# Corner weights in PSUM, all squares on the scalar engine, the offset chain spread over tiles, and a looped gather program that copies its indices per tile

## What is computed

```python
x = x + _L0_conv_ref(_gn(x), W, b)                    # attention over all pixels: relu(f'f)^2, values normalised
x = x + _L1_conv_ref(_gn(x), offset_w, offset_b, dcn_w)   # modulated deformable convolution, 9 taps
x = x + _L2_conv_ref(_gn(x), ...)                     # diagonal LSTM in both directions
x = x + _L3_conv_ref(_gn(x), ...)                     # adaptive deformable convolution, 9 taps
```

## Time and profile before

| | before |
|---|---|
| runs, us | 14,493.77, 14,497.03, 14,500.39 (median 14,497.03) |
| profiled execution, us | 14,491.91; span of the trace 14,489.8 |
| PE busy | 8644.1 us, 60% |
| POOL busy | 8632.6 us, 60% |
| DVE busy | 6885.5 us, 48% |
| ACT busy | 4883.7 us, 34% |

### The profile page before, as it was taken

One profiled execution on the slowest core, in us unless ns is written; L12 is line 12 of the kernel. 1 busy time (PEld: TensorE's weight loads), 2 busy tenths in 40 slices (PEclk: granted clock), 3 DMA queues, 4 the chain that ended last, 5 costly groups with the idle time before them and its releaser, 6 DMA issues. The chain is left out here.

```text
span 14489.8 us, 110898 instructions
## 1 busy us (share of the span) xinstructions
PE 8644.1 (60%) x26294; PEld 3625.3 (25%) x26294; DVE 6885.5 (48%) x8889; ACT 4883.7 (34%) x7671; POOL 8632.6 (60%) x7465
## 2 busy tenths in 40 slices
PE   7888887878788787852188888233332323333322
PEld 2333333323233333321044444111111111111111
DVE  3444545454544545444344444444454454444444
ACT  4444443434344444431178888111111111111100
POOL 0176775757576675767500000477777777777777
PEclk9899898989899898975599999555555555555555
DMA  0122222222222222227522222634343443433332
GB/s 7 37 84 78 87 82 82 82 81 82 81 82 81 83 84 80 85 84 175 139 56 56 58 56 56 127 98 115 97 114 101 114 114 99 115 98 98 97 94 88
DMA packets 1168915, 1277.68 MB, mean 88 GB/s; under 512 B 795967, under 2 KB 924415, under 8 KB 1164671
## 3 DMA queue, kind: packets, MB, share of 16 engines
q0 software_dynamic: 338688, 925.30, 21.6%
q1 hardware_dynamic: 815710, 347.84, 10.5%
q10 hardware_dynamic: 14368, 3.21, 0.1%
HBM read 1080.00 MB, written 195.82 MB: 88 GB/s over the span
## 5 line engine op out<-in xcount | busy, mean ns | idle before, releaser
L423 POOL DMA_INDIRECT b_gathered<-table,b_iu x3528 | 4451.0, 1262 | 1323.9 <-issue 988.5
L423 POOL DMA_INDIRECT d_gathered<-table,d_iu x3528 | 4114.3, 1166 | 1279.1 <-issue 1049.6
L518 PE MATMUL PS<-b_key 128*128 (+1 forms) x5600 | 2557.9, 583 | 18.2 <-ACT b_weights L694 7.3
L543 PE MATMUL PS<-ident,d_sample 128*128 128x128 f32 (+1 forms) x1960 | 504.2, 421 | 3229.5 <-DVE d_sample L893 2996.5
L694 ACT ACTIVATE b_weights<-PS 128x896 f32<-128x896 f32 (+1 forms) x1400 | 1281.8, 916 | 2296.3 <-PE PS L518 1886.3
L531 PE MATMUL PS<-b_weights,b_values 128*64 128x448 f32 (+1 forms) x5600 | 1466.7, 591 | 619.0 <-DVE b_weights L873 585.0
L881 DVE TENSOR_TENSOR d_gathered<-d_gathered,d_w 128x2304 f32<-128x2304 f32 x392 | 1002.6, 2558 | 1494.8 <-DMA d_gathered<-table,d_iu 1451.8
L881 DVE TENSOR_TENSOR b_gathered<-b_gathered,b_w 128x2304 f32<-128x2304 f32 x392 | 1002.2, 2557 | 1395.2 <-DMA b_gathered<-table,b_iu 1391.5
L704 ACT ACTIVATE d_sampleT<-PS 128x512 f32<-128x512 f32 x392 | 233.2, 595 | 3346.0 <-PE PS L543 2676.3
L518 PEld LDWEIGHTS PS<-b_key 128*128 128x128 f32 (+1 forms) x5600 | 994.5, 197 | 1330.5 <-issue 1325.1
L873 DVE TENSOR_TENSOR b_weights<-b_weights 128x896 f32<-128x896 f32 x672 | 731.2, 1088 | 1185.2 <-ACT b_weights L694 943.3
(11 more groups left out here) (224 smaller groups left out, 9533.6 us busy)
## 6 DMA issues: line engine op xcount, KB each, us to landing
b_gathered<-table,b_iu POOLq DMA_INDIRECT x3528
d_gathered<-table,d_iu POOLq DMA_INDIRECT x3528
l_x_and_h<-xs SPq DMA_DIRECT2D x224, 224.0 KB, 3.6
hs<-l_hT SPq DMA_DIRECT2D x224, 224.0 KB, 2.4
d_h<-hs SPq DMA_DIRECT2D x32, 1554.0 KB
table<-b_table_rows SPq DMA_DIRECT2D x208, 128.0 KB, 1.9
table<-d_table_rows SPq DMA_DIRECT2D x208, 128.0 KB
xs<-b_key SPq DMA_DIRECT2D x14, 1568.0 KB
```

Source lines behind the costliest of these rows:

```text
L423: pool.indirect_dma_start(GB[:, g, k, :], None, tables[b], bass.IndirectOffsetOnAxis(ap=ix, axis=0)).then_inc(gathered[g], 16)
L518: mm = pe.matmul(PS[0:keys(k), 2 * (k % S_BUFS) + a, 0:CH], KEY[:, a, k * P:k * P + keys(k)], KEY[:, a, bass.ds(j * CH, CH)], start=True, ...
L543: mm = pe.transpose(PS[0:n, 5 + s // 4, (s % 4) * P:(s % 4 + 1) * P], S[:, t % 2, s * P:s * P + n], K.ident[:, :])
```

## The change

1. `W4`, the corner weights, was an SBUF tile for all chunks of a pair, written by the last four instructions of `positions`. It is now one chunk's worth in PSUM bank 6. `corner_weights` fills it at the head of each chunk, from `LO`, `HI`, `WL`, `WH`, which stay as they are until the next chunk's positions.
2. All squares go to ACT; DVE's are gone.
3. `positions` is split into `place`, `split` and `index_rows`. In the chunk loop they stand ahead of steps 6, 8 and 10 of the fused stage (a tile is three steps) and of steps 12, 14 and 16 of the second stage, where PE's and ACT's part also moved behind the first tiles.
4. POOL's seven chunks are a loop instead of written out, and ahead of each tile POOL copies its nine indices per partition from `IU` into a fixed place `IC`, from which the gathers read. The MEMSET is gone. A copy's wait asks for the samples of the same tile one chunk ago.
5. Since bank 6 is taken, other PSUM banks are renumbered.

```diff
-        W4 = [sb(f"w4_{n}", [P, PREPS * CT, 4]) for n in range(NB)]
+        W4 = PS[:, 6, 0:4 * CT].rearrange("p (r q) -> p r q", q=4)
...
-                for j in range(NCH):
+                with pool.Fori(0, NCH) as j:
                     c = m * NCH + j
                     wait_apart(pool, coords_ready, q + j + 1)
                     for t in range(TPC):
                         g = t % G_BUFS
-                        if att:
-                            pool.memset(DRAIN[:, :], 0.0).then_inc(pool_drained, 1)
-                            wait_apart(pool, pool_drained, c * TPC + t + 1)
+                        wait_apart(pool, samples_ready, c * TPC + t + 1)
+                        pool.tensor_copy(IC[:, t * TAPS:(t + 1) * TAPS], IU[b][:, bass.ds((j * TPC + t) * TAPS, TAPS)])\
+                            .then_inc(chunk_ix, 1)
+                        pool.wait_ge(chunk_ix, c * TPC + t + 1)
                         wait_apart(pool, samples_ready, c * TPC + t + 1 - BACK[t] + TPC)
                         for k in range(TAPS):
-                            n = (j * TPC + t) * TAPS + k
-                            ix = IU[b][:, n:n + 1]
+                            ix = IC[:, t * TAPS + k:t * TAPS + k + 1]
...
-                if k in ACT_SQ:
-                    act.wait_ge(relu_done, c * QT + k + 2)
-                    act.activation(AW[0:n, k % A_BUFS], AW[0:n, k % A_BUFS], ACT.Square).then_inc(weights_act, 1)
+                act.wait_ge(relu_done, c * QT + k + 2)
+                act.activation(AW[0:n, k % A_BUFS], AW[0:n, k % A_BUFS], ACT.Square).then_inc(squared, 1)
...
+            def corner_weights(c, q):
+
+                v.wait_ge(coords_ready, q + 2)
+                flat = "p t k -> p (t k)"
                 for n, (yw, xw) in enumerate(((LO, WL), (HI, WL), (LO, WH), (HI, WH))):
-                    ins = v.tensor_tensor(W4[b][:, rows, n], yw[:, 0].rearrange(flat), xw[:, :, :].rearrange(flat), ALU.mult)
-                ins.then_inc(coords_ready, 1)
-                assert own.n == OWN, (own.n, OWN)
+                    ins = v.tensor_tensor(W4[:, :, n], yw[:, 0].rearrange(flat), xw[:, :, :].rearrange(flat), ALU.mult)
+                ins.then_inc(corners_ready, 1)
+                v.wait_ge(corners_ready, c + 1)
...
-                            if k == 6 and not last:
-                                positions(q + j, j + 1, b)
-                            elif k == 6 and nxt:
-                                positions(q + j, 0, nxt[1])
+                            if k == 0:
+                                corner_weights(c, q + j - 1)
+                            to = (j + 1, b) if not last else (0, nxt[1]) if nxt else None
+                            first = 6 if att else 12
+                            if to and k == first:
+                                own = Count(q + j, OWN)
+                                place(q + j, to[0], own)
+                            if to and k == first + 2:
+                                split(own)
+                            if to and k == first + 4:
+                                index_rows(*to, own)
...
-                        if i is not None and k in DVE_SQ:
-                            square(i * NCH + j, k)
```

More of the change, by code:

```diff
@@ L222, in sampled_layer @@
         ROW_BANK = 2 if att else 0
+        OM_BANK = 7 if att else 2
+        OMT_BANK = 5 if att else 3
         EARLY = range(6)
@@ L234, in sampled_layer @@
         USES = [len([t for t in range(TPC) if t % G_BUFS == b]) for b in range(G_BUFS)]
-        ACT_SQ = [k for k in range(QT) if k % 2 == 0]
-        DVE_SQ = [k for k in range(QT) if k % 2]
         assert 3 * TPC + 2 < QT
@@ L524, in add_values @@
                     pe.wait_ge(xin_ready, c + 1)
-                if k in ACT_SQ:
-                    wait_apart(pe, weights_act, c * len(ACT_SQ) + ACT_SQ.index(k) + 1)
-                else:
-                    wait_apart(pe, weights_dve, c * len(DVE_SQ) + DVE_SQ.index(k) + 1)
+                wait_apart(pe, squared, c * QT + k + 1)
                 n = keys(k)
@@ L536, in turn_samples @@
             def turn_samples(c, t, q):
-                if t == 0:
+                if att and t == 0:
                     pe.wait_ge(omT_ready, q + 1)
@@ L557, in sampling_chunk @@
             def sampling_chunk(m, b, q, nxt, j, last):
-                if nxt or not last:
-                    pe.wait_ge(y_ready, m * NCH + j + 1)
+                ahead = nxt or not last
+                if ahead:
+                    if att:
+                        pe.wait_ge(y_ready, m * NCH + j + 1)
                     offsets(q + j, 0 if last else j + 1, nxt[1] if last else b)
-                    turn_offsets(q + j)
+                    if att:
+                        turn_offsets(q + j)
                 for t in range(TPC):
-                    turn_samples(m * NCH + j, t, q + j if nxt or not last else q + j - 1)
+                    turn_samples(m * NCH + j, t, q + j if ahead else q + j - 1)
+                    if ahead and not att and t == 1:
+                        pe.wait_ge(omT_ready, q + j)
+                        turn_offsets(q + j)
                     if att and t == TPC - 2:
@@ L619, in take_offsets @@
                 act.wait_ge(omT_mm, q + 1)
-                act.activation(OM[:, C:C + CH], PS[0:C, 7, 0:CH], ACT.Identity, bias=OB[:, :]).then_inc(om_ready, 1)
+                act.activation(OM[:, C:C + CH], PS[0:C, OM_BANK, 0:CH], ACT.Identity, bias=OB[:, :]).then_inc(om_ready, 1)
             def take_turned(q):
@@ L704, in evict_samples @@
                 act.activation(ST[:, 0:4, t * P:(t + 1) * P], PS[:, 5, :].rearrange("p (s f) -> p s f", s=4), ACT.Copy)
-                act.activation(ST[0:C, 4, t * P:(t + 1) * P], PS[0:C, 6, 0:P], ACT.Copy).then_inc(samplesT_ready, 1)
+                act.activation(ST[0:C, 4, t * P:(t + 1) * P], PS[0:C, 7, 0:P], ACT.Copy).then_inc(samplesT_ready, 1)
             def sampling_chunk(m, b, q, nxt, j, last):
-                if nxt or not last:
+                ahead = nxt or not last
+                if ahead and att:
                     take_offsets(q + j)
@@ L716, in sampling_chunk @@
                     evict_samples(m * NCH + j, t)
+                    if ahead and not att and t == 0:
+                        take_offsets(q + j)
+                    if ahead and not att and t == 2:
+                        take_turned(q + j)
                     if att and t == TPC - 2:
@@ L783, in normalize_for_sampling, with own_step, place @@
                                 ALU.subtract, ALU.mult).then_inc(g_ready, 1)
-            def positions(q, jj, b):
-                own = Count(q, OWN)
-                rows = slice(0, CT) if isinstance(jj, int) else bass.ds(jj * CT, CT)
+            def own_step(own, ins):
+                ins.then_inc(own_dve, 1)
+                v.wait_ge(own_dve, own())
+            def place(q, jj, own):
                 tiles = slice(0, TPC) if isinstance(jj, int) else bass.ds(jj * TPC, TPC)
-                def did(ins):
-                    ins.then_inc(own_dve, 1)
-                    v.wait_ge(own_dve, own())
+                did = lambda ins: own_step(own, ins)
                 v.wait_ge(omT_ready, q + 1)
@@ L826, in positions, with split @@
                 did(v.tensor_scalar(POS[:, :], POS[:, :], 0.0, float(PW - 1), ALU.max, ALU.min))
+            def split(own):
+                did = lambda ins: own_step(own, ins)
                 did(v.tensor_copy(FI[:, :], POS[:, :]))
@@ L868, in keys_and_values, with weigh_corners @@
                     v.tensor_tensor(VAL[:, px], VAL[:, px], RLEN[:, 1, :], ALU.mult).then_inc(kv_ready, 1)
-            def square(c, k):
-                v.wait_ge(relu_done, c * QT + k + 2)
-                w = AW[0:keys(k), k % A_BUFS]
-                v.tensor_tensor(w, w, w, ALU.mult).then_inc(weights_dve, 1)
-            def weigh_corners(c, j, t, b):
+            def weigh_corners(c, t):
                 g = t % G_BUFS
@@ L938, in chunk @@
                 def chunk(j, last):
-                    for k in range(QT if i is not None else 3 * TPC):
-                        if m is not None and k < 3 * TPC:
+                    for k in range(3 * TPC):
+                        if m is not None:
                             c, t = m * NCH + j, k // 3
```

46 lines of the change are left out of this document (26 added, 20 removed).

## The result

The changed kernel takes 15,077.12 us (median of 3 runs, 15,048.98 to 15,144.39) against 14,497.03: ratio 1.0409, 95% interval 1.0355 to 1.0464. It is slower, where 13,680 was forecast. The profiled execution took 15,048.98 us.

A forecast was written before the change was run, and what follows sets the result against it. DVE's two-SBUF-input instructions were taken to decide POOL's pace. Fused -659, tail -60 and second stage -101, together -820 from 14,491.9, gave 13,672, forecast as 13,680 us; own range 13,560 to 13,830, with rival B 13,540 to 13,960.

The forecast's parts named there:

- What holds a gather: All sampling stages: DVE instructions with two SBUF inputs hold gathers until 0.82 us behind their end; a PSUM operand frees them.
- The copy: Ahead of each tile: POOL's index copy leaves a gap of 1.05 us, +0.05 us a fused tile, mostly swallowed in second stage.
- Rival C: Ahead of each tile: the copy's gap exceeds 2.07 us, one more gather is held, 14,680 us in all; chance 0.04.
- The tail stage: Last pair's sampling, 49 tiles: 14.2 us a tile falls to 12.96, -60 us.
- POOL never waits for its consumers: Fused stage: waits for DVE samples are 19.9 us in all, so 5105 us is POOL's own pace, decided by DVE.
- 343 tiles of free gathers: Fused stage: 343 x (10.96 + 1.05 + 0.87), with small terms 4446 us against 5105, -659.
- rival B: Fused stage: PE becomes the bound, 85.6 us a chunk without gaps; at 96 us the total is 13,945; chance 0.13.
- sign of B: Fused stage: POOL waiting for samples would show that PE has become the bound.
- The pair heads: Outside the sampling stages, with first attention pass, skew and LSTM: they hold no gather and the change hardly touches them.
- Rival A: All sampling stages: the multiplication holds gathers wherever its weights lie, 14.3 us a tile, 14,775 us in all; chance 0.08.
- Squares on ACT: Attention: 672 DVE squares of 1088 ns become 950 ns on ACT, hidden below PE; POOL loses the waits on them.
- The second stage: 392 tiles of sampling without attention: 5164 us against 5265, -101, with 17 us of sample waits and none for coordinates.

The follow-up runs named there:

- one pause a tile: Changed kernel plus, in every tile, a one-element MEMSET and a wait for it ahead of the sixth gather: 14,044 us, ratio 0.973.
- without multiplication: Kernel before with the multiplication by the corner weights left out, a one-element copy standing for it: 15,753 us.
- spread chain alone: Changed kernel with weights in SBUF, squares shared by ACT and DVE, POOL's old program; coordinate chain still spread over the chunk: 14,383 us, ratio 0.993.
- weights in SBUF: Changed kernel with the corner weights in SBUF again, one buffer filled per chunk, everything else kept: 15,012 us, ratio 1.037.
- two pauses: Changed kernel plus, in every tile, a one-element MEMSET and a wait ahead of the fourth and of the seventh gather: 14,178 us.

## Why the prediction was wrong, step by step

- **What holds a gather: right.** The multiplication with its PSUM operand takes 2.55 us and gathers under it 0.94 (9875.05); the addition from 9881.96 to 9883.32 holds the gather from 9882.31, which ends at 9884.13, 0.81 us behind. The Trainium skill, page "SBUF — State Buffer", § Who interferes with whom, has both halves of this, a DVE instruction with at most one SBUF input does not contend with GpSimd; the trace now agrees with the second half as well.
- **The copy: right.** 0.20 us and 0.85 of idle, the gap of 1.05. Some copies are held as well, which brings their mean to 0.22 and 0.27 us. Rival C is out.
- **The tail stage: right,** -71 us where -60 was forecast. PE is busy for 177 us of its 640 there. The -60 took 14.2 us for the tile before; the prediction's own 716 us for 49 tiles are 14.6, and with them it is -81.
- **The step that failed** is "POOL never waits for its consumers ... DVE is the one that decides POOL's pace", and from it the fused stage as 343 tiles of free gathers: -659 forecast, +605 measured. The wait for samples, 19.9 us before, was put at nothing, and it is 1346.9 us; POOL's own pace fell by 862. The prediction took PE's time (85.6 us a chunk, rival B's floor, whose terms add up to 84.8) to be independent of what POOL does. It is not: with the gathers freed the same PE work takes 116 us a chunk, and POOL then waits for samples, the prediction's own sign of B. The pair heads, which "the change hardly touches", cost 121 us more of POOL's waiting. Rival A had the sign, but its mechanism did not occur: nothing under the multiplication was held.
- **Squares on ACT, "cost nothing":** as work they are hidden, 55.0 us of ACT a chunk where 58 was worked out. Taken from DVE, where they held POOL, they cost 475 us in the kernel before and 685 in the changed one (6362 against 5677). The prediction priced them by what they free and not by what they protect.
- **Rival B** was nearest to the truth, with 96 us a chunk from PE's bubbles, but as forecast it gives 13,945. Its 96 us a chunk is about what one pause a tile gives (94.0, with PE busy for 86.19 of it), once PE is on time; that kernel's 14,044 us lies near 13,945. "POOL runs up to four tiles ahead, which is why I don't expect it" had it backwards: in the kernel without multiplication it is while POOL runs ahead, 33 gathers in a row, that PE's result stays out.
- **The second stage:** -101 forecast, +21 measured. Its gathers are as short as forecast (1040 ns), and POOL's own pace, 5027 us, is 120 below the 5147 of the sum. The waits were mis-sized: samples at 17 us, measured 97.0; coordinates "a few us ..., none in the sum", measured 158.0, up to 24.1 at once. Both are gone with one pause a tile, so they come of PE's lateness, as in the 26-us wait above. With the spread chain alone both of its small terms are right.
- **The clock** fell with it: 0.88 granted in the window from 3108.4, where PE is busy for 92.64 of 116.6 us, and 0.96 with one pause, where it is busy for 86.19 of 94.0. The work is the same (285 and 281 matmuls on record), so PE's lower clock is some 6 us of the 23 between the two windows.

## What to carry to other kernels

Before freeing an engine from a hold, ask who works during the hold. When a consumer is idle and the profile can't name who released it, or when two waiting instructions start together long after the producer's record has ended, look whether the producer's result came later than its record says. Where GpSimd issues indirect gathers in long rows beside matmuls, try a one-element MEMSET with a wait every five gathers or so: it takes 0.9 us where a gap of 0.30 stood, and in the fused stage it brought the tile from 116.6 / 7 = 16.7 to 94.0 / 7 = 13.4 us. In the second stage it made things 81 us longer (5366 against 5285). Choose it stage by stage.

## What the runs showed of the hardware

- What waits for matmuls starts late beside long rows of indirect gathers: 47.5 us after the start of a convolution whose records cover 10 (33 gathers in a row), 27.4 us after the start of transposes of 1.3. The Trainium skill, page "SBUF — State Buffer", § Who interferes with whom, says that "PE and ACT never wait on anyone". ACT's instructions keep their length here (the relu 914 ns, 916 before). For PE, that its consumers get its results up to 37.5 us after its records' end is measured, and a plan has to go by that. Whether PE itself waits is another question, and the next point speaks against it.
- The semaphore's update is what comes late: in the wait for the transposes above it stands at 9902.28. The trace also holds the times of the updates (not quite all: 2542 of 2800 for scores and value products in the changed kernel). There, 656 of these updates come more than 1 us behind the end of PE's record; in the kernel before it is 95, without multiplication 794, with weights in SBUF 385, with one pause 118, with two pauses 3. 155 follow the one before on the same semaphore by less than 0.6 us, some by 0.06, though the matmuls behind one update take PE 0.75 us or more; before it is 15, with two pauses none. The profile models the ends of matmuls, but this spacing doesn't depend on them. So in these, at least, the earlier work was done well before its update came. Of the updates by ACT (relu) and DVE (samples) none is more than 1 us behind its instruction's end in any of these kernels.
- What goes with PE on time: gathers held by two-input DVE instructions, or 0.9 us of another POOL instruction often enough. Rows of three gathers left the relu 2.5 us of remote idle in the whole run, of five and four 34 us. A single break a tile was not always enough: with the copy's pause and a held gather in each tile (weights in SBUF) the relu has 1168 us of it, and in the changed kernel two pauses and a held gather leave the transposes unreported until 9902.30. Where between rows of five and of nine the limit lies wasn't tried.
- It does not depend on the bytes moved (a quarter of them: the same), and it comes without any DVE instruction that reads weights in PSUM (no multiplication; weights in SBUF). What it is in a gather that holds up PE's updates and not ACT's or DVE's is open, and so is whether PE computes late as well. The Trainium skill, page "DMA: Bandwidth & Descriptors", § Terms, places the descriptor rings of GpSimd's DMAs in SBUF; that traffic to them is in the way would be one explanation, and no run here shows it. Gathers with fewer rows at the same pace would be the next thing to try; that wasn't tried.
